# The end of the quantizer in a four-block kernel on one core: other PSUM banks and other engines for its last three units

## The reference

```python
x = embeddings.transpose(0, 2, 3, 1).reshape(-1, e)

def stage(res, cb):
    d = jnp.sum(res * res, axis=1, keepdims=True) - 2.0 * jnp.einsum('ne,ke->nk', res, cb) + jnp.sum(cb * cb, axis=1)
    idx = jnp.argmin(d, axis=1)
    q = cb[idx]
    return (res - q, q)
_, qs = jax.lax.scan(stage, x, codebooks)
```

## Time and profile before

| | us |
|---|---|
| median of 3 runs | 1495.66 (1492.65 to 1497.45) |
| the profiled execution's own time | 1497.99 |
| its span, first to last instruction | 1495.9 |
| outside the span | 2.1 |
| mean granted TensorE clock | 0.933 of full speed |

### The profile page before, as it was taken

One profiled execution on the slowest core, in us unless ns is written; L12 is line 12 of the kernel. 1 busy time (PEld: TensorE's weight loads), 2 busy tenths in 40 slices (PEclk: granted clock), 3 DMA queues, 4 the chain that ended last, 5 costly groups with the idle time before them and its releaser, 6 DMA issues. The chain is left out here.

```text
span 1495.9 us, 30285 instructions
## 1 busy us (share of the span) xinstructions
PE 1229.4 (82%) x10814; PEld 505.9 (34%) x10814; DVE 1170.9 (78%) x3667; ACT 871.4 (58%) x1169; POOL 954.5 (64%) x727
## 2 busy tenths in 40 slices
PE   4798988988988988988968899958888667776675
PEld 1222222222222222222215666626656411121111
DVE  6999999999999999999976455562222358887886
ACT  2687888888888888888843444320000046676654
POOL 5699888888888898898820332321000059989885
PEclk7799999999999999999979999989999959889877
DMA  7111211111121111111104433410000030202001
GB/s 175 52 44 44 68 46 55 45 52 60 45 68 45 53 48 57 55 44 58 44 30 101 106 89 86 103 41 18 2 1 2 23 73 1 48 1 62 1 15 29
DMA packets 65894, 74.43 MB, mean 50 GB/s; under 512 B 17776, under 2 KB 55920, under 8 KB 65744
## 3 DMA queue, kind: packets, MB, share of 16 engines
q1 hardware_dynamic: 64544, 70.68, 17.3%
q10 hardware_dynamic: 1200, 1.82, 0.5%
HBM read 42.21 MB, written 2.62 MB: 30 GB/s over the span
## 5 line engine op out<-in xcount | busy, mean ns | idle before, releaser
L515 POOL TENSOR_SCALAR l_onehot<-l_ib,c_cols 128x512 bf16<-128x512 uint8 x248 | 385.1, 1565 | 9.6 <-DMA l_ib<-l_indices 9.6
L669 DVE CUSTOM_DVE_ANT_0 l_scored<-ps,l_gain 128x256 f32<-128x256 f32 x1024 | 373.5, 416 | 14.2 <-ACT l_gain L423 13.4
L423 ACT ACTIVATE l_gain<-ps 128x1024 f32<-128x1024 f32 (+1 forms) x320 | 272.6, 852 | 144.9 <-PE ps L298 144.8
L298 PE MATMUL ps<-l_ct_slot,l_res 32*128 32x512 f32 x2048 | 340.1, 607 | 0.0
L637 DVE FIND_INDEX8 l_idx<-l_top,l_scored 128x8 uint16<-128x1024 f32 (+1 forms) x320 | 326.4, 1020 | 0.0
L1896 POOL TENSOR_TENSOR l_isum<-l_term 128x512 f32<-128x512 f32 x160 | 204.8, 1311 | 40.2 <-DVE l_term L2000 25.9
L306 PE MATMUL ps<-l_onehot,l_cbp_slot 128*32 128x512 bf16 x3072 | 217.1, 391 | 5.9 <-ACT l_signed L449 3.1
L293 PE MATMUL ps<-l_csq,l_row_slot 32*128 32x512 bf16 x1024 | 128.7, 394 | 84.0 <-DVE l_top L669 78.8
L1626 PE MATMUL ps<-l_isum,w_l_w_dsc 64*64 64x512 f32 x640 | 104.4, 713 | 59.8 <-POOL l_isum L1896 58.8
L1816 ACT ACTIVATE ps<-ps,w_l_minus 128x512 f32<-128x512 f32 x192 | 118.6, 661 | 51.2 <-DVE l_term L2006 35.1
L398 ACT ACTIVATE l_away<-l_ib,c_cols 128x1024 f16<-128x1024 uint8 x126 | 143.8, 1141 | 0.4 <-DMA l_ib<-l_indices 0.4
(11 more groups left out here) (214 smaller groups left out, 1604.3 us busy)
## 6 DMA issues: line engine op xcount, KB each, us to landing
l_ib<-l_indices SPq DMA_DIRECT2D x64, 512.0 KB, 3.7
l_xi<-l_xt SPq DMA_DIRECT2D x120, 128.0 KB
l_xi<-l_xz SPq DMA_DIRECT2D x36, 144.2 KB, 3.1
X<-in_x SPq DMA_DIRECT2D x16, 128.0 KB, 6.6
out<-X SPq DMA_DIRECT2D x16, 128.0 KB, 2.2
l_xr<-l_xt SPq DMA_DIRECT2D x30, 64.0 KB
l_ct<-in_codes_t SPq DMA_DIRECT2D x4, 448.0 KB, 12.1
l_ct_slot<-l_ct SPq DMA_DIRECT2D x7, 256.0 KB, 3.7
```

Of the source, the lines that this page charges most:

```text
L298: pe.matmul(ps[:, at + m, :], res[rows, i, P * tt:P * (tt + 1)], ct_slot[rows, par, :], start=False, stop=True, skip_group_check=True).the ...
L423: nc.scalar.activation(gain[:, at:at + len(tiles), :], ps[:, at:at + len(tiles), PAIRED:], ACT.Relu).then_inc(s_gain, 1)
L515: nc.gpsimd.tensor_scalar(spread(onehot[:, v % 2, g, 0, :]), low(v % 2, g, 1), iota[:, 0:1], None, ALU.is_equal).then_inc(s_near, 1)
L669: nc.vector.tensor_tensor_reduce(out=scored[:, (SLOTS * w + k) % 3, m * PAIRED:(m + 1) * PAIRED], in0=ps[:, at + m, :PAIRED], in1=gain[:, ...
```

## The change

- `signed` has two buffers, by v % 2. The sign of v waits until v-2 is settled.
- The five drain periods and their loop are gone from PE, ACT and DVE. In their place each engine has a list for the end, written out.
- PE: step, middle and ones product of the units 61, 62 and 63, and the ones product of 60, have banks of their own (`STEP_BANK`, `MIDDLE_BANK`, `SIDE_BANK`; the score banks are free by then). The middle no longer waits for the copy of the step, and the near chunks of step and middle are picked before the far ones.
- ACT makes all four far one-hots of unit 62 and two of unit 63 (before: two of each).
- POOL settles the units 59, 60 and 61 and takes the units 58 to 61 out of X (`leave(2)` to `leave(5)`), behind `wc`. DVE keeps `leave` of 56, 57, 62 and 63, the settling of 62 and 63, and all middles and products of 61 to 63.
- DVE starts on the one-hots of 62 directly behind `turn`; `next_moments` comes before the one-hots of 63, `next_image` before the middle of 63.

The diff, cut to its core:

```diff
 KEPT = 4
-DRAIN = 5
 POOL_UNITS = ALL - 2
-LAST_HOTS = G + 2
+STEP_BANK = {ALL - 3: PICK, ALL - 2: 1, ALL - 1: 4}
+MIDDLE_BANK = {ALL - 3: 6, ALL - 2: 2, ALL - 1: 5}
+SIDE_BANK = {ALL - 4: 0, ALL - 3: 3, ALL - 2: PICK, ALL - 1: 6}
 LOWEST = -3.0e38
...
-        signed = t("signed", [P, HALF])
+        signed = t("signed", [P, 2, HALF])
...
-            return START + min(v + 1, POOL_UNITS) * 2 + max(v + 1 - POOL_UNITS, 0)
+            return START + min(2 * (v + 1), 2 * ALL - 1)
...
+            def side(v, bank=PICK):
+
+                pe.wait_ge(s_product, START + v + 1)
+                pe.matmul(ps[:, bank, :], block_ones[:], product[:, v % 2, :],
+                          start=True, stop=True).then_inc(s_side, 1)
...
-                        pe.wait_ge(s_product, START + late + 1)
-                        if mid is not None:
-                            pe.wait_ge(s_off, START + mid + 1)
-                        else:
-                            pe.wait_ge(s_sign, START + late)
-                        pe.matmul(ps[:, PICK, :], block_ones[:], product[:, late % 2, :],
-                                  start=True, stop=True).then_inc(s_side, 1)
-
+                        pe.wait_ge(s_off, START + mid + 1)
+                        side(late)
+
+            v = ALL - 3
+            pe.wait_ge(s_near, START + G * (v + 1))
+            pe.wait_ge(s_off, START + v)
+            pe.wait_ge(s_sign, START + v - 1)
+            pick(v, 0, 0, STEP_BANK[v])
+            pe.wait_ge(s_far, far_ready(v))
+            pick(v, 0, 1, STEP_BANK[v]).then_inc(s_steps, 1)
             pe.wait_ge(s_top, START + ALL * TILES)
+            pick(v, 1, 0, MIDDLE_BANK[v])
+            pick(v, 1, 1, MIDDLE_BANK[v]).then_inc(s_middle, 1)
+            side(v - 1, SIDE_BANK[v - 1])
+            for v in (ALL - 2, ALL - 1):
+                pe.wait_ge(s_last, START + G * (v - POOL_UNITS + 1))
+                pick(v, 0, 0, STEP_BANK[v])
+                pick(v, 1, 0, MIDDLE_BANK[v])
+                pe.wait_ge(s_far, far_ready(v))
+                if v == ALL - 1:
+                    pe.wait_ge(s_last, START + 2 * G + 2)
+                pick(v, 0, 1, STEP_BANK[v]).then_inc(s_steps, 1)
+                pick(v, 1, 1, MIDDLE_BANK[v]).then_inc(s_middle, 1)
+                side(v - 1, SIDE_BANK[v - 1])
+            side(ALL - 1, SIDE_BANK[ALL - 1])
...
+            def copy_step(v, bank=PICK):
+
+                act.wait_ge(s_steps, START + v + 1)
+                if v >= KEPT:
+                    act.wait_ge(s_signed, START + v - (KEPT - 1))
+                nc.scalar.copy(step[:, v % KEPT, :], ps[:, bank, :]).then_inc(s_step, 1)
+
+            def sign(v, bank=PICK):
+
+                act.wait_ge(s_side, START + v + 1)
+                if v >= 2:
+                    act.wait_ge(s_res, START + v - 1 + UNITS)
+                nc.scalar.activation(signed[:, v % 2, :], ps[:, bank, :], ACT.Sign,
+                                     bias=const["minus_tiny"][:]).then_inc(s_sign, 1)
+
+            def reach(v):
+
+                act.wait_ge(s_ib[v % 2], ib_ready(v))
+                if v >= 2:
+                    act.wait_ge(s_middle, START + v - 1)
...
+            copy_step(ALL - 3, STEP_BANK[ALL - 3])
+            reach(ALL - 2)
+            distance(ALL - 2, 0)
+            far(ALL - 2, 0)
+            sign(ALL - 4, SIDE_BANK[ALL - 4])
+            distance(ALL - 2, 2)
+            far(ALL - 2, 2)
+            reach(ALL - 1)
+            act.wait_ge(s_far, far_ready(ALL - 2))
+            distance(ALL - 1, 2)
+            copy_step(ALL - 2, STEP_BANK[ALL - 2])
+            far(ALL - 1, 2)
+            act.wait_ge(s_next, START + 3)
+            nc.scalar.activation(nstd[:, 0:1], nmv[:, 0:1, 1], ACT.Sqrt, bias=eps[:]).then_inc(s_next_std, 1)
+            sign(ALL - 3, SIDE_BANK[ALL - 3])
+            copy_step(ALL - 1, STEP_BANK[ALL - 1])
+            sign(ALL - 2, SIDE_BANK[ALL - 2])
+            sign(ALL - 1, SIDE_BANK[ALL - 1])
...
+            def settle(v):
+
+                i = v % UNITS
+                pool.wait_ge(s_sign, START + v + 1)
+                pool.sem_inc(s_alone, 1)
+                nc.gpsimd.tensor_tensor(signed[:, v % 2, :], signed[:, v % 2, :], step[:, v % KEPT, :],
+                                        ALU.mult).then_inc(s_signed, 1)
+                pool.wait_ge(s_signed, START + v + 1)
+                pool.sem_inc(s_alone, 1)
+                nc.gpsimd.tensor_tensor(res[:, i, :], res[:, i, :], signed[:, v % 2, :],
+                                        ALU.subtract).then_inc(s_res, 1)
+
+            def leave(i):
+
+                pool.wait_ge(s_res, START + ALL + i + 1)
+                pool.sem_inc(s_alone, 1)
+                xi = X[:, i * HALF:(i + 1) * HALF]
+                nc.gpsimd.tensor_tensor(xi, xi, res[:, i, :], ALU.subtract).then_inc(s_out_pool, 1)
+
+            settle(ALL - 5)
+            leave(2)
+            settle(ALL - 4)
+            leave(3)
+            leave(4)
+            settle(ALL - 3)
+            leave(5)
             pool.wait_ge(s_wc, START + 1)
+            pool.wait_ge(s_out_pool, START + 4)
...
+            def middle(v):
+
+                i = v % UNITS
+                dve.wait_ge(s_middle, START + v + 1)
+                nc.vector.tensor_tensor(res[:, i, :], res[:, i, :], ps[:, MIDDLE_BANK[v], :],
+                                        ALU.add).then_inc(s_off, 1)
+                dve.wait_ge(s_off, START + v + 1)
+                dve.wait_ge(s_step, START + v + 1)
+                dve.wait_ge(s_product, START + v)
+                nc.vector.tensor_tensor(product[:, v % 2, :], res[:, i, :], step[:, v % KEPT, :],
+                                        ALU.mult).then_inc(s_product, 1)
+
             def settle(v):
 
-                i = v % UNITS
+                i, n = v % UNITS, 2 * (v - (ALL - 2))
                 dve.wait_ge(s_sign, START + v + 1)
-                nc.vector.tensor_tensor(signed[:], signed[:], step[:, i % KEPT, :], ALU.mult).then_inc(s_signed, 1)
-                dve.wait_ge(s_signed, START + v + 1)
-                nc.vector.tensor_tensor(res[:, i, :], res[:, i, :], signed[:], ALU.subtract).then_inc(s_res, 1)
+                nc.vector.tensor_tensor(signed[:, v % 2, :], signed[:, v % 2, :], step[:, v % KEPT, :],
+                                        ALU.mult).then_inc(s_tail, 1)
+                dve.wait_ge(s_tail, START + n + 1)
+                nc.vector.tensor_tensor(res[:, i, :], res[:, i, :], signed[:, v % 2, :],
+                                        ALU.subtract).then_inc(s_tail, 1)
 
             def leave(i):
 
-                dve.wait_ge(s_res, START + ALL + i + 1)
+                if i < UNITS - 2:
+                    dve.wait_ge(s_res, START + ALL + i + 1)
+                else:
+                    dve.wait_ge(s_tail, START + 2 * (i - (UNITS - 2)) + 2)
...
-            for i in range(DRAIN):
-                w = ALL + i
-                early, fresh, mid, done = (back(w, n) for n in (1, 2, 3, 5))
-                if early is not None:
-                    dve.wait_ge(s_top, START + early * TILES + TILES)
-                    dve.sem_inc(s_alone, 1)
-                    find(early, SLOTS - 1)
-                    turn(early)
-                if i == 0:
-                    for e in range(UNITS - DRAIN):
-                        leave(e)
-                if i == 1:
-                    settle(done)
-                if fresh is not None:
-                    dve.wait_ge(s_ib[fresh % 2], ib_ready(fresh))
-                    dve.wait_ge(s_middle, START + fresh - 1)
-                    for g in range(G):
-                        hot(fresh, g, 0)
-                    for g in range(LAST_HOTS - G):
-                        hot(fresh, g, 1)
-                if i != 1:
-                    settle(done)
-                if mid is not None:
-                    add_middle(mid)
-                    dve.wait_ge(s_off, START + mid + 1)
-                    dve.wait_ge(s_product, START + mid)
-                    nc.vector.tensor_tensor(product[:, mid % 2, :], res[:, mid % UNITS, :], step[:, mid % KEPT, :],
-                                            ALU.mult).then_inc(s_product, 1)
-                if i == 1:
-                    next_moments()
-                if i == 2:
-                    next_image()
-                leave(done % UNITS)
-
-            dve.wait_ge(s_out, START + UNITS)
+            dve.wait_ge(s_top, START + ALL * TILES)
+            dve.sem_inc(s_alone, 1)
+            find(ALL - 1, SLOTS - 1)
+            turn(ALL - 1)
+            dve.wait_ge(s_ib[0], ib_ready(ALL - 2))
+            dve.wait_ge(s_middle, START + ALL - 3)
+            for g in range(G):
+                hot(ALL - 2, g, 0)
+            middle(ALL - 3)
+            leave(0)
+            leave(1)
+            next_moments()
+            dve.wait_ge(s_ib[1], ib_ready(ALL - 1))
+            dve.wait_ge(s_middle, START + ALL - 2)
+            for g in range(G):
```

(41 more changed lines are left out.)

38 lines of the change are left out of this document (15 added, 23 removed).

## The result

| | before | changed |
|---|---|---|
| median of 8 runs each, same chip | 1496.64 us (1492.65 to 1499.57) | 1487.13 us (1483.48 to 1489.91) |
| the profiled execution, its span | 1497.99, 1495.9 us | 1488.25, 1485.3 us |
| mean granted TensorE clock | 0.933 | 0.941 |
| last transpose on DVE to the first instruction of block L1 | 759.86 to 792.41: 32.55 us | 759.96 to 783.51: 23.55 us |

The ratio is 0.9934, 95% interval 0.9917 to 0.9950: faster by 9.5 us (7.5 to 12.4 by the interval), where 5.7 were forecast (1490.0, range 1481 to 1495). In the two traces the stage's end, from the last transpose on, is 9.0 us shorter; the block starts 8.9 us earlier. The remaining 1.7 us of the spans' difference lie behind the stage (703.5 us before, 701.8 after). The same remainder is 698.8 to 706.2 us in the profiled runs of the experiments, which don't touch it: 1.7 us lie well within that scatter.

The account below looks back on a forecast made before the run. The stage's end was taken as a chain of latencies with no engine full. Gain 6.5 us with turns, 4.9 us with low clock, taken as 5.7: 1490.0 us against the median of 1495.66, range 1481 to 1495.

Parts of the forecast that it names:

- early ones product: Stage's end on PE: the ones product of 60 runs before 761 instead of starting at 766.30.
- long DVE instructions: Stage's end on DVE: settling, `leave` and one-hot instructions take 1.3 to 2 us where POOL is busy.
- low clock around 774 to 782: TensorE near the stage's end: granted clock 0.50 there; gain between 4.9 and 6.5 us, taken as 5.7.
- one-hots of 63 spread over 6 us: DVE, stage's end: these six start from about 771 and end at 777.2, held up by POOL.
- the ring: Stage's end before: engines wait for each other through bank 7, three turns of some 9 us each.
- 9.1 us of waits for POOL: DVE at the stage's end: summed waits for POOL, 0.9 + 1.3 + 0.6 + 5 x 1.3.
- three times 1.28 us: One-hots of 63 on DVE: POOL's settling of 61 and `leave(5)` fall among all six, which end at 777.2.
- The walk: Stage's end with DVE and POOL taking turns: next block at 785.9 instead of 792.4, 6.5 us gained before the clock.
- One-hots do not meet POOL: Rival, DVE's one-hots undisturbed: next block at 781.6, gain 10.8 us, 1484.9 us; chance 0.17.
- No contention: Rival, DVE and POOL never wait for each other: next block at 776.85, gain 15.6 us, 1480.1 us; chance 0.12.
- eaten at half clock: Rival, TensorE at 1.2 GHz through the eight passes: next block at 791.2, gain 1.3 us, 1494.4 us; chance 0.13.
- slower rival: Rival, clock still low in the next block, at L925 and L943: 6.0 us slower, 1501.7 us; chance 0.08.

Follow-up runs that it names:

- e3: Changed kernel with POOL idle behind `wc` and DVE in the order of the kernel before; 23.55 us from last transpose to L1, ratio 0.9927.
- e4: Kernel before plus only POOL settling 59 to 61 and `leave` of 58 to 61; 31.3 us from last transpose to L1, ratio 0.9976.
- e2: Changed kernel with POOL idle behind `wc`, its settlings and `leave` on DVE, changed DVE order kept; 22.8 us to L1, ratio 0.9925.
- e1: Changed kernel with POOL's ten end instructions cut to one column of 512; 16.8 us from last transpose to L1, ratio 0.9879.
- e7: Changed kernel plus three useless matmuls on PE behind the ones product of 60; 23.6 us from last transpose to L1, ratio 0.9938.
- e10: Kernel of POOL settling 59 only, plus ACT making all four far one-hots of 63; 22.4 us from last transpose to L1, ratio 0.9922.
- e5: Changed kernel with POOL settling only 59, the rest of the tail on DVE; 21.5 us from last transpose to L1, ratio 0.9922.
- e6: Changed kernel reordered: POOL settles 59 and 61, takes out 60 and 61; one-hots of 63 before `next_moments`; 20.6 us to L1, ratio 0.9927.

## Why the prediction was right, and where it was off

Right in its mechanism and too small in its size, by 3.2 us of the trace (8.9 for 5.7). The miss was near the edge of what the prediction itself called wrong: block L1 started at 783.51, and before 783 would have been wrong. Of its signs, the early ones product and the long DVE instructions came; the low clock around 774 to 782 and the one-hots of 63 spread over 6 us did not.

- **Bounds and start.** The stretch up to 756.6 is unchanged; the ones product of 60 came at 759.37 (forecast 759.4), its sign at 760.91 (761.0). Unbinding the ring is the gain, as e3 and e4 show; e3 keeps the second `signed` buffer and ACT's and PE's lists with the banks.
- **POOL's share.** Its ten instructions took what was forecast, 1.28 us, or a wait for DVE more (1.56 and 1.60 us, and 3.42 for the two `leave` of 59 and 60). That DVE loses by it was forecast; that nothing is left of it net was not said, and e2 and e3 show it.
- **Turns, the term that was mis-sized.** The sum gives 9.1 us of waits for POOL (its terms add up to 9.2 with the 1.28 us of each); e1 puts them at 6.8. The one-hots of 62 (1.9 us, forecast 2.2), the product of 61 (0.4, 0.6) and `leave` of 56 and 57 (2.2 over the 1.28 that e1 shows for the pair, 2.6) were near, and DVE came to the one-hots of 63 at 770.17 instead of 771.0. Then the step "three times 1.28 us" failed: POOL cost them 2.06 us. The picks that need only the four near ones start at 771.86, so those four had passed undisturbed; the two that were left alternated with two POOL instructions, not three. I had counted POOL's instructions and not the one-hots still to come. The third, `leave(5)`, started at 774.55, when the last one-hot was ending, and cost the product of 62 0.4 us. The one-hots ended at 774.65 instead of 777.2, and DVE's end at 782.7 instead of 785.1 follows from that.
- **The clock.** Forecast at 0.50 around 774 to 782 us, cost 0 to 1.6 us, taken as 0.8. It was 1.00 there. The walk had PE idle for 6.5 us, from 767.5 to 774.0, because it took the picks of 62 at full clock and put POOL among the near one-hots of 63. The ones product of 61 ended at 769.16, behind picks at half clock, and the near picks came at 771.86, so the gap was 2.69 us. The clock was low from 763.9 to 767.3, where it stretches the picks of 62 to 4.46 us; e7 shows no gain from its return, and DVE was in its turns with POOL all the while. The Trainium skill warns that waits between bursts let the gate fall (TensorE: Matmul & The Clock Gate, "HAM oscillation"); the trace agrees for the gap of 3.16 us ahead of the picks of 62, and not for the one of 2.69. Nor do the other runs make the length of a gap the whole reason: in e7 24 picks ran at full clock (1.48 us) behind 3.27 us without work, in e3 48 at half clock (4.46 us) behind 1.38.
- **The sum.** 0.8 us from the earlier steps, 1.4 from the one-hots of 63 (3.8 less 2.06) less the product of 62 (0.4), 0.2 in the steps behind them, 0.8 from the clock: the 3.2 us. The last PE pass ended at 783.25, 0.5 us behind the last `leave`, as forecast (0.4).
- **Rivals.** "One-hots do not meet POOL" would have given 781.6 for the block's start, which is nearer to the measured 783.5 than the forecast's 786.7, but e1 rules its reason out: its number came near because the turns were overrated, not because they were absent. "No contention" is what e1 shows, 776.5, near the 776.85 worked out. The gain was not eaten at half clock. The slower rival's mechanism is real (e2, e10), and was seen only behind 3.78 us of idle PE ahead of L1; the changed kernel has 0.30 there, and e5 kept the full clock behind 2.09 (ten passes in 4.53 us).

The runs do not part the banks from the second `signed` buffer, the near-first picks and ACT's two more one-hots, which stayed together in e3. So that the banks are the part that does it is argued from the waits, not shown. Nor do they settle the 1.7 us behind the stage.

## What to carry to other kernels

When an end of a stage is a ring of short steps, look first for the shared buffer that closes it: here a bank of its own for each step, with the lists that use them, brought all of the gain, and moving work off an engine in the ring brought 1.2 us by itself. Moving elementwise work from DVE to POOL was worth only the part that lay beside DVE's finds (e5), beside DVE instructions which read PSUM or gather statistics (e6), or beside an idle DVE; beside products, subtractions and one-hots it cost DVE as much as it took off (6.8 us for 6.2). Keep PE's last idle stretch of a block short, since its price is paid in the next block (1.2 us in e2): matmuls put there to hold the clock must end with the last engine, not before it.

## What the runs showed of the hardware that was not expected

- A POOL instruction on one column has to wait for its turn as well: 0.74 us instead of 0.19 in e1, beside a DVE instruction of 0.81 us.
- DVE loses less than the whole POOL instruction at each meeting: two meetings cost the one-hots of 63 2.06 us, where POOL's two took 1.60 (with its own wait; 1.28 undisturbed) and 1.26.
- TensorE fell to 1.2 GHz at the start of L1 behind 3.78 us without work (e2, e10: ten passes in 6.23 us) and stayed at 2.4 GHz behind the changed kernel's 0.30 and e5's 2.09 (4.53 us).
- The clock differs between executions where the program does not: the picks of 61 took 2.77 us in e2 and 4.46 in e3, behind the same PE work and the same 1.38 us without any.
